# Two ConvLSTM recurrences: packing their split-precision products into seven 128-row operands

## What is computed

```
def step(carry, xr):
    h, c = carry
    inp = jnp.concatenate([xr, h], axis=1)
    gates = lax.conv_general_dilated(inp, w_mid, (1,), 'SAME', dimension_numbers=dn) + b[None, :, None]
    i, f, g, o = jnp.split(gates, 4, axis=1)
    c2 = jax.nn.sigmoid(f) * c + jax.nn.sigmoid(i) * jnp.tanh(g)
    h2 = jax.nn.sigmoid(o) * jnp.tanh(c2)
    return ((h2, c2), h2)
```

## Time and profile before

| | us |
|---|---|
| median of three runs | 2120.07 |
| the profiled execution, own time | 2124.06 |
| its span, first to last instruction | 2122.2 |
| recurrences, both layers, first to last sigmoid | 545.3 + 545.3 |
| PE busy in the span | 1832.6 (86%) |
| DVE busy | 1387.2 (65%) |
| ACT busy | 1066.5 (50%) |
| POOL busy | 765.1 (36%) |

### The profile page before, as it was taken

The page is one execution under the profiler, slowest core; times in us unless marked ns, Lnnn a source line. Parts: engine busy times, 40 slices in busy tenths (PEclk is TensorE's granted clock), DMA queues, the critical chain, the costliest instruction groups (busy, mean ns, idle before and its releaser), DMA issues. The chain is left out here.

```text
span 2122.2 us, 43782 instructions
## 1 busy us (share of the span) xinstructions
PE 1832.6 (86%) x16306; PEld 1197.3 (56%) x16306; DVE 1387.2 (65%) x2552; ACT 1066.5 (50%) x1961; POOL 765.1 (36%) x581
## 2 busy tenths in 40 slices
PE   6979179999999998459999999998503999999999
PEld 5535157777777775137777777776101455555555
DVE  5539968888888886658888888888541333333334
ACT  1116147777777775737777777776611222222220
POOL 2010055666666653036666566564029000000000
PEclk9989689999999999769999999999756999999999
DMA  2769420000000000930000000000760011101100
GB/s 74 250 193 201 105 54 22 22 24 22 22 24 22 22 24 13 168 97 23 24 22 23 23 22 24 22 22 9 125 170 0 3 32 32 33 18 33 32 18 25
DMA packets 74138, 111.26 MB, mean 52 GB/s; under 512 B 11248, under 2 KB 30560, under 8 KB 74032
## 3 DMA queue, kind: packets, MB, share of 16 engines
q1 hardware_dynamic: 74032, 109.65, 20.7%
HBM read 71.87 MB, written 37.75 MB: 52 GB/s over the span
## 5 line engine op out<-in xcount | busy, mean ns | idle before, releaser
L668 PE MATMUL gates_l<-xh_l,w_hi_l 112*112 112x512 f32 x3072 | 819.7, 402 | 106.3 <-DVE keep_l L730 106.3
L668 PEld LDWEIGHTS gates_l<-xh_l,w_hi_l 112*112 112x112 f32 x3072 | 537.9, 175 | 304.8 <-issue 107.2
L644 POOL TENSOR_TENSOR xh_l<-xf_l,xh_l 48x512 fp32r<-48x512 f32 x256 | 359.9, 1406 | 281.8 <-ACT xh_l L687 281.3
L668 PE MATMUL gates_l<-xh_l,w_lo_l 112*112 112x512 f32 x1536 | 450.4, 402 | 0.0
L639 POOL TENSOR_TENSOR xh_l<-hs,xh_l 48x512 fp32r<-48x512 f32 x254 | 303.6, 1195 | 173.7 <-DVE hs L759 173.7
L668 PEld LDWEIGHTS gates_l<-xh_l,w_lo_l 112*112 112x112 f32 x1536 | 270.0, 176 | 98.0
L1132 PE MATMUL b_dw<-b_hid,b_diag 32*32 32x512 f32 x9120 | 312.4, 599 | 0.0
L699 ACT ACTIVATE gate_if_l<-gates_l 112x512 f32<-112x512 f32 x256 | 153.4, 599 | 246.0 <-PE gates_l L668 246.0
L739 DVE TENSOR_TENSOR keep_l<-gate_if_l,cell_l 48x512 f32<-48x512 f32 x256 | 175.5, 686 | 140.7 <-ACT gate_if_l L699 140.7
L1132 PEld LDWEIGHTS b_dw<-b_hid,b_diag 32*32 32x32 f32 x9120 | 186.4, 103 | 114.4 <-issue 46.9
L748 DVE TENSOR_TENSOR cell_l<-keep_l,add_l 48x256 f32<-48x256 f32 x512 | 196.8, 428 | 26.6
(11 more groups left out here) (148 smaller groups left out, 1288.3 us busy)
## 6 DMA issues: line engine op xcount, KB each, us to landing
xf_l<-rows SPq DMA_DIRECT2D x256, 96.0 KB, 2.0
hs<-rows SPq DMA_DIRECT2D x32, 384.0 KB, 10.6
rows<-hs SPq DMA_DIRECT2D x32, 384.0 KB, 5.1
xr<-in_x_rows SPq DMA_DIRECT2D x24, 256.0 KB, 2.7
xc<-in_x_cols SPq DMA_DIRECT2D x24, 256.0 KB, 3.0
mixed<-stage SPq DMA_DIRECT2D x24, 256.0 KB, 3.0
edged<-stage SPq DMA_DIRECT2D x24, 256.0 KB, 3.2
mixed_sb<-mixed SPq DMA_DIRECT2D x32, 192.0 KB, 7.3
```

The source lines that it names most:

```text
L644: pool.tensor_tensor(xh[far[d]:far[d] + C, d, s, 1, :, 1:W + 1], xf[far[d]:far[d] + C, s, :].rearrange("p (b w) -> p b w", b=B), xh[far[d] ...
L668: mm = nc.tensor.matmul(ps[d][m][0:K, :], weight[:, d, m, t, :], xh[0:K, d, s, part, :, t:t + W], start=(first and t == 0), stop=(last and ...
```

## The change

It rearranges the rows of the matmuls' operands in `lstm_scans`, so that they use all 128 partitions.

- The gap rows of both halves now carry the first 32 channels of the rounded x; the last 16 channels stand in an operand of their own, `xc`, in three shifted copies, twice, with two rows of ones for the bias. The low part of x stands in the tile with the high part of h, and a copy of the high part of h in the tile with its low part. The weights hold a high or a low value row by row, by a mask. So there are seven operands (`xc`, three taps of `HI`, three taps of `LO`) and 14 matmuls per step instead of 18.
- The rounded x is made once per row for both directions, by one ACT instruction on 112 partitions into `xs`, after direction 1's tanh of the cell. SP then spreads it with four SBUF-to-SBUF DMAs per step.
- ACT copies the rounded state of the other direction into `LO` (`copy_state`) after the sigmoid of o, and tanh of g stays in PSUM. PE's last six matmuls wait for the copy as well as for `h_lo`.
- DVE's add works in place in PSUM, and its cell update is one instruction instead of two halves. The tanh of the cell, still in two halves, waits for the whole.
- x is loaded three rows ahead, both directions together.
- At a layer's start the weights are 128 x 3136 values instead of 112 x 1344; they are loaded into rows of `hs` and split on DVE by two copies and four multiply-adds with the mask. ACT begins only when DVE has done this.

The lines of `lstm_scans` that are added, with some that stay, eight columns to the left; the lines that they replace stand in the kernel above. `layout` on the host builds the weights and the mask to match.

```diff
     sems.append(nc.alloc_semaphore(name + tag))
     return sems[-1]
+NCH = 7
+NW = 2 * NCH * 2 * K
+WROWS = -(-NW // BW)
+raw = hs[:, H // 2:H // 2 + WROWS, :].rearrange("p a n -> p (a n)")[:, 0:NW]
+w = sb("w", [P, 2, NCH, 2, K], F32R)
+mask = sb("mask", [P, 2, 2])
 xf = sb("xf", [P, 2, BW])
+xs = sb("xs", [P, 2, FLAT + 2 * LEAD], F32R)
+xh = sb("xh", [P, 2, 2, 2, FLAT], F32R)
+xc = sb("xc", [P, 2, 2, FLAT], F32R)
 gate_if = sb("gate_if", [P, 2, BW])
+gate_o = sb("gate_o", [P, 2, BW])
+keep = sb("keep", [P, BW])
+begun = sb("begun", [P, 8])
 cell = ctx.enter_context(nc.psum_tensor("cell" + tag, [P, 2, BW], F32))
...
+def padded(ap):
+    return ap.rearrange("p (b w) -> p b w", b=B)
+def inner(ap):
+    return padded(ap)[:, :, 1:W + 1]
+def wide(ap):
+    return ap.rearrange("p (b w) -> p b w", b=B)
+def x_rows(r, rows):
+    return xs[rows, r, LEAD:LEAD + FLAT]
 with nc.Block() as block:
     @block.sync
     def _(sp):
+        sp.dma_start(raw, D[weights]).then_inc(w_loaded, 16)
+        sp.dma_start(mask[:, :, :], D["l_mask"]).then_inc(w_loaded, 16)
+        def load(row_f, row_b, r):
+            sp.dma_start(xf[far[0]:far[0] + C, r, :], rows_in[row_f]).then_inc(x_in[r], 16)
+            sp.dma_start(xf[far[1]:far[1] + C, r, :], rows_in[row_b]).then_inc(x_in[r], 16)
+        def spread(d, s):
+            for a in range(2):
+                some = x_rows(s, slice(far[d] + a * GAP, far[d] + (a + 1) * GAP)).bitcast(F32)
+                sp.dma_start(xh[a * HALF + C:(a + 1) * HALF, d, s, :, :].bitcast(F32), some.unsqueeze(1).broadcast_to([GAP, 2, FLAT])
+                             ).then_inc(x_spread[d][s], 16)
+            rest = xs[far[d] + 2 * GAP:far[d] + C, s, LEAD - 1:LEAD - 1 + FLAT].bitcast(F32)
+            shifts = bass.AP(rest.tensor, rest.offset, [list(rest.ap[0]), [1, 3], [1, FLAT]])
+            for c in range(2):
+                sp.dma_start(xc[3 * GAP * c:3 * GAP * (c + 1), d, s, :].bitcast(F32), shifts).then_inc(x_spread[d][s], 16)
+        sp.wait_ge(xf_cleared, 1)
+        for r in range(2):
+            load(r, H - 1 - r, r)
+        sp.wait_ge(cleared, 3)
         for s in range(2):
+            sp.wait_ge(x_hi, s + 1)
+            for d in range(2):
+                spread(d, s)
+        sp.wait_ge(x_lo[0], 1)
+        sp.wait_ge(x_lo[1], 1)
+        load(2, H - 3, 0)
+        def step(k, more=2):
             for s in range(2):
+                done, ahead, split = (held(sp, 2 * k + (s + n)) for n in (1, 2, 3))
+                row_f, row_b = split, held(sp, k * -2 + (H - 4 - s))
+                if s < more:
+                    sp.wait_ge(x_lo[0], ahead)
+                    sp.wait_ge(x_lo[1], ahead)
+                    load(row_f, row_b, 1 - s)
+                for d in range(2):
+                    sp.wait_ge(gates[d][1], done)
+                    if d == 0:
+                        sp.wait_ge(x_hi, split)
+                    spread(d, s)
+        with sp.Fori(0, H // 2 - 2) as k:
+            step(k)
+        step(H // 2 - 2, more=1)
     @block.gpsimd
     def _(pool):
+        pool.memset(xs[:, :, :].bitcast(F32), 0.0).then_inc(cleared, 1)
...
         def split_lo(t, d, s):
+            f = far[d]
+            pool.wait_ge(x_hi, t + 1)
+            if not (isinstance(t, int) and t < 2):
+                pool.wait_ge(gates[d][1], t - 1)
+            pool.tensor_tensor(inner(xh[f:f + C, d, s, HI, :]), wide(xf[f:f + C, s, :]),
+                               inner(x_rows(s, slice(f, f + C))).bitcast(F32), ALU.subtract).then_inc(x_lo[d], 1)
+        pool.wait_ge(cleared, 3)
+        pool.wait_ge(xf_cleared, 1)
         for s in range(2):
             for d in range(2):
                 split_lo(s, d, s)
+        def step(k, last=False):
+            for s in range(2):
+                for d in range(2):
+                    if not last:
+                        split_lo(2 * k + (s + 2), d, s)
+                    if not last or s == 0:
+                        state_lo(2 * k + s, 2 * k + s if d == 0 else k * -2 + (H - 1 - s), d, s)
+        with pool.Fori(0, H // 2 - 1) as k:
             step(k)
         step(H // 2 - 1, last=True)
     @block.tensor
     def _(pe):
+        pe.wait_ge(w_ready, 4)
+        pe.wait_ge(cleared, 3)
         with pe.Fori(0, H // 2) as k:
             for s in range(2):
                 for d in range(2):
+                    def chunk(m, q, tile, lo, first=False, last=False):
+                        return nc.tensor.matmul(ps[d][m][0:K, :], w[:, d, q, m, :], padded(tile)[:, :, lo:lo + W],
+                                                start=first, stop=last)
+                    pe.wait_ge(x_spread[d][s], SPREAD * k + SPREAD)
+                    pe.wait_ge(sig_if[d], 2 * k + (s + 1))
+                    pe.wait_ge(sig_o[d], 2 * k + (s + 1))
+                    pe.wait_ge(cells[d], 2 * k + (s + 1))
+                    for m in range(2):
+                        chunk(m, 0, xc[:, d, s, :], 1, first=True)
+                    pe.wait_ge(x_lo[d], 2 * k + (s + 1))
+                    pe.wait_ge(h_hi[d], 2 * k + (s + 1))
+                    for m in range(2):
                         for t in range(3):
+                            chunk(m, 1 + t, xh[:, d, s, HI, :], t)
+                    pe.wait_ge(h_copy[d], 2 * k + (s + 1))
+                    pe.wait_ge(h_lo[d], 2 * k + (s + 1))
                     for m in range(2):
+                        for t in range(3):
+                            mm = chunk(m, 4 + t, xh[:, d, s, LO, :], t, last=(t == 2))
+                        mm.then_inc(gates[d][m], 1)
     @block.scalar
     def _(act):
+        act.wait_ge(cleared, 3)
         for d in range(2):
+            act.wait_ge(h_hi[d], 1)
+            act.wait_ge(cells[d], 1)
+        def split_hi(t, r):
+            act.wait_ge(x_in[r], 16 * t - 16 * r + 32)
+            if not (isinstance(t, int) and t < 2):
+                for d in range(2):
+                    act.wait_ge(x_spread[d][r], (t - r) * (SPREAD // 2))
+                    act.wait_ge(x_lo[d], t - 1)
+            nc.scalar.activation(inner(x_rows(r, slice(0, K))), wide(xf[0:K, r, :]), ACT.Copy).then_inc(x_hi, 1)
+        def copy_state(t, d, s):
+            n, f = near[d], far[d]
+            act.wait_ge(h_hi[d], t + 1)
+            nc.scalar.activation(inner(xh[f:f + C, d, s, LO, :]), inner(xh[n:n + C, d, s, HI, :]).bitcast(F32),
+                                 ACT.Copy).then_inc(h_copy[d], 1)
+        for r in range(3):
+            split_hi(r, r % 2)
+        copy_state(0, 0, 0)
+        def step(k, more=2, last=False):
+            for s in range(2):
+                for d in range(2):
+                    n, f = near[d], far[d]
+                    act.wait_ge(gates[d][0], 2 * k + (s + 1))
+                    nc.scalar.activation(gate_if[0:K, d, :], ps[d][0][0:K, :], ACT.Sigmoid).then_inc(sig_if[d], 1)
+                    act.wait_ge(gates[d][1], 2 * k + (s + 1))
+                    nc.scalar.activation(ps[d][1][n:n + C, :], ps[d][1][n:n + C, :], ACT.Tanh).then_inc(tanh_g[d], 1)
+                    nc.scalar.activation(gate_o[f:f + C, d, :], ps[d][1][f:f + C, :], ACT.Sigmoid).then_inc(sig_o[d], 1)
+                    if d == 0:
+                        copy_state(2 * k + s, 1, s)
+                    elif not (last and s == 1):
+                        copy_state(2 * k + (s + 1), 0, 1 - s)
+                    act.wait_ge(cells[d], 2 * k + (s + 2))
+                    for j, part in enumerate(parts):
+                        nc.scalar.activation(tanh_c[f:f + C, j, 0:PART], cell[f:f + C, j, 0:PART],
+                                             ACT.Tanh).then_inc(tanhs[d], 1)
+                if s < more:
+                    split_hi(2 * k + (s + 3), 1 - s)
+        with act.Fori(0, H // 2 - 2) as k:
+            step(k)
+        step(H // 2 - 2, more=1)
+        step(H // 2 - 1, more=0, last=True)
+    @block.vector
+    def _(dve):
+        nc.vector.memset(xf[32:64, :, :], 0.0).then_inc(xf_cleared, 1)
+        nc.vector.memset(xh[:, :, :, :, :].bitcast(F32), 0.0).then_inc(cleared, 1)
+        nc.vector.memset(xc[96:128, :, :, :].bitcast(F32), 1.0).then_inc(cleared, 1)
+        for d in range(2):
+            f = far[d]
+            nc.vector.memset(cell[f:f + C, :, 0:PART], 0.0).then_inc(cells[d], 1)
+        dve.wait_ge(w_loaded, 32)
+        per_d = NCH * 2 * K
+        for d in range(2):
+            nc.vector.tensor_copy(w[:, d].rearrange("p a b c -> p (a b c)"), raw[:, d * per_d:(d + 1) * per_d]
+                                  ).then_inc(w_hi, 1)
+        for d in range(2):
+            dve.wait_ge(w_hi, d + 1)
+            for q, chunks in enumerate((slice(0, 1), slice(1, 4))):
+                part = w[:, d, chunks].rearrange("p a b c -> p (a b c)")
+                whole = raw[:, d * per_d + chunks.start * 2 * K:d * per_d + chunks.stop * 2 * K]
+                nc.vector.scalar_tensor_tensor(part, part.bitcast(F32), mask[:, d, q:q + 1], whole, ALU.mult, ALU.add
```

(40 more changed lines are left out.)

151 lines of the change are left out of this document (38 added, 113 removed).

## The result

| | before | after |
|---|---|---|
| median, us | 2120.71 (4 runs) | 2100.19 (4 runs, 2100.04 to 2103.59) |
| profiled execution, own time and span | 2124.06, 2122.2 | 2100.29, 2098.5 |
| recurrences, first to last sigmoid | 545.3 + 545.3 | 516.5 + 516.7 |

The ratio is 0.9905, interval 0.9889 to 0.9921: 20 us, 1% faster, where 8.6 us were forecast.

What follows compares the result with a forecast made beforehand. PE was taken to set the pitch, with DVE close behind and next to bind. Recurrences -33.9, layer starts +24.8 and tail +0.5 summed to -8.6 us, giving 2111.5 us, range 2070 to 2165.

Steps and rivals of the forecast that it cites:

- DVE's chain: Recurrence step: keep, add, cell, first tanh, state, output, back to keep sum to 4.025 us and set the new pitch.
- the form without overlap: Output to next keep in DVE's chain: keep starts only after output ends, 0.71 us; with overlap 0.60.
- The split of x: ACT's split before the sigmoid delays every second keep, making that step 0.27 us longer; mean pitch 4.16.
- The start: Each layer's start, to its first sigmoid: longer weight loading, splitting and spreads; +24.8 us over two layers, 8 to 18 each.
- the 11.4 worked out: Layer start: first sigmoid at 28.1 us, 11.4 later than before; 1 us was then added for PE's lower clock.
- The tail: Behind a layer's last sigmoid: grows by the tanh that no longer overlaps, 0.27 us each, +0.5 in all.
- No late spread: SP's spreads in the loop, wanted three steps (12 us) after issue, were priced at nothing.
- rival 3: Spreads late in the loop, small packets all on SP's queue: pitch 4.5, 2197 us; chance 0.06.
- rival 4: PE falls to the 1.2 GHz clock level from idling 0.8 us in each step: 2579 us; chance 0.04.
- Rival 5: PE stays the bound in the recurrences, if DVE's chain could shorten to 3.5: 1943 us; chance 0.03.
- Rival 2: DVE's add and cell cost more PSUM to PSUM: slower, 2162 us at 0.1 each, bound 2246; chance 0.17.
- Rival 1: Split and holds vanish in the loop as ACT runs ahead: pitch 4.02 or less, 2076 us; chance 0.15.

Runs made afterwards that it cites:

- e4: Not the computation: only ScalarE copies of 512 columns, eight in a row per pattern; start to start 0.48 us on one partition start, 0.60 where it changes.
- e5: Changed kernel with ACT's in-loop split of x cut from 64 columns to one, leaving most of x out: 2094.76 us, ratio 0.9874.
- e7: Changed kernel with two matmuls more per step, 16, placed before the wait for the copy: 2097.14 us, ratio 0.9886, pitch 4.07.
- e6: Kernel before with four of six high-input-by-low-weight products left out, 14 matmuls a step, nothing else changed: 2316.45 us, ratio 1.0919.
- e8: Changed kernel with tanh of g and DVE's add back in SBUF tiles: 2422.12 us, ratio 1.1417, pitch 5.36.
- e9: Kernel before with e6's four products left out, and tanh of g and add kept in PSUM: 1980.67 us, ratio 0.9343, pitch 3.76.

## Why the prediction was right or wrong

The direction was right, and the mechanism: DVE's chain takes over from PE, and a longer start takes part of the gain back. The size was off, by more in its terms than the sum shows, for they went opposite ways: against the spans the pitch gave 23.5 us more than forecast, the starts cost 6.0 more, and what lies around them 2.3 more. That the total came out no further off is in part luck.

- **DVE's chain, right.** 4.025 forecast; the steps take 4.04 and 4.07. Add and cell were put at 0.695 and measured 0.697. Output to the next keep takes 0.72 (321.29 to 322.01), thus the form without overlap, 0.71. I had taken the choice that the Trainium skill's rule for VectorE backs, and the trace agrees. POOL's subtraction of x went down to 1.19, as forecast.
- **The split of x, the step that failed.** The prediction put it on the path to every second keep; the runs show it hidden. "So every second step is 0.27 longer: mean (4.025 + 4.295)/2 = 4.16 us." Behind it stands the sum 0.69 + 0.03 + 0.63 + 0.03 + 0.60 + 0.07 = 2.05 from the first tanh to the keep. Measured: 326.09 - 324.26 = 1.83 (1.85 in the mean), where the steps without a split take 1.79. The pair of tanh takes 0.61, not 0.69, since the whole cell is there and the second half has no wait in it; so the split starts 0.64 after the first tanh, not 0.72. And the sigmoid starts 0.54 after the split, not 0.66. These two make 0.20 of the 0.22. I added up durations with a gap of 0.03, while ScalarE's instructions with the same partition starts overlap by 0.1 (e4). I had weighed just such a rule for VectorE, and not asked whether ScalarE has one. e5 shows the price of the split: 0.01 a step instead of 0.135. With the pitch at 4.07 instead of 4.16 the recurrences gave -57.4 instead of -33.9.
- **The start, mis-sized the other way.** 12.4 a layer were forecast, 15.4 measured. DVE was ready when forecast, the weights were not late. But I had priced SP's issue of a spread at 7.5/16 = 0.47, the upper end of the plain loads, and it takes 0.59 to 0.79, 10.8 us for the 16. Row 2's load is queued behind them all, and took 3.5 from issue to ACT instead of 2.9. These two, 3.3 and 0.6, are the 3.9 by which the start exceeds the 11.4 worked out. The 1 us that I added for PE's lower clock does not show ahead of the first sigmoid. The granted clock was 0.50, the 1.2 GHz level, from 298 to 302 us, and the first two steps took 8.61 us together, 0.5 more than two later ones. Over two layers +30.8 instead of +24.8.
- **The tail.** +0.9 a layer instead of +0.27; too small to settle.
- **No late spread, right**, and rival 3 falls. **The clock, right**: 1.00 with PE idle in every step, and rival 4 falls.
- **Rival 5** (PE stays the bound) falls by e7.
- **Rival 2** (PSUM at both ends costs more) falls: 0.697. But its opposite should have stood in the text. I used POOL's hold of the add to explain 0.81 in place of 0.69, and counted the relief as 0.1. I did not ask what that hold would do once PE no longer set the rhythm. e6 and e8 show it: without the move to PSUM the same matmul cut ends at 2316 or 2422. The Trainium skill (SBUF — State Buffer, "Who interferes with whom") has the rule: a VectorE instruction with two SBUF inputs shares a read interface with GpSimd under a lock, one with a single SBUF input doesn't. The trace of e6 agrees: the add ends 0.54 after POOL's subtraction, and keep stays at 0.69.
- **Rival 1** (split and holds vanish) had its mechanism half right: the split is hidden, but DVE's holds between output and keep stay. What it gave for the whole, 2076, missed since the pitch stayed 0.05 above its 4.02 (12 us) and the starts cost more (6 us).

What stays open: the 2.3 us in the projection of that one execution, and the tail. That the clash in e6 and e8 locks itself is read from their timelines; a kernel that shifts POOL's work in time, without changing where operands lie, was not tried. What keeps the split from overlapping the tanh ahead of it is open too.

## What to carry to other kernels

When an engine is relieved, ask of every instruction of the next bound which neighbour it will now meet: a hold worth 0.1 us in one phase was worth 322 us (e8 against the changed kernel) and 336 us (e6 against e9) in another, and moving one input of add and cell to PSUM removed it. Add up an engine's chain by start-to-start times, and note for each pair whether the partition starts change: in the changed kernel the pairs that changed them never overlapped, on ScalarE or on VectorE. And read the busy share of an engine with care: PE at 90% had at least half a microsecond in each 4 to give away, while DVE at 85%, in a chain with the tanh on ScalarE, set the pitch.
